# Three input stages: the power one round behind the variance, deeper rings, the mask read in place

## The reference, cut to what matters

```python
x = x + L0(_gn(x));  x = x + L1(_gn(x));  x = x + L2(_gn(x));  x = x + L3(_gn(x))

# L3, the others alike (L0 and L1 have no mask)
z_norm = layer_norm(z, norm_g, norm_b)
left  = (z_norm @ Wa + ba) * sigmoid(z_norm @ Wga + bga)
right = (z_norm @ Wb + bb) * sigmoid(z_norm @ Wgb + bgb)
left, right = left * mask[..., None], right * mask[..., None]
z_out = einsum('bikc,bjkc->bijc', left, right)
z_out = layer_norm(z_out, norm_out_g, norm_out_b)
return (z_out @ Wo + bo) * sigmoid(z_norm @ Wgo + bgo)
```

## Time and profile before

| | us |
|---|---|
| median of 3 runs | 1777.76 (1776.29 to 1778.16) |
| profiled execution | 1780.16 |
| its span, first to last instruction | 1778.4 |
| busy: PE, DVE, ACT, POOL | 1331.0, 1383.3, 1167.7, 1001.5 |

### The profile page before, as it was taken

How to read it: one execution, slowest core, us unless ns; L and a number is a source line. 1 busy time by engine, 2 the same in 40 slices (tenths; PEclk the granted TensorE clock), 3 DMA queues, 4 the chain that set the end, 5 groups by cost and what they waited for, 6 DMA issues and landing times.

```text
span 1778.4 us, 30667 instructions
## 1 busy us (share of the span) xinstructions
PE 1331.0 (75%) x9712; PEld 797.9 (45%) x9712; DVE 1383.3 (78%) x3708; ACT 1167.7 (66%) x2680; POOL 1001.5 (56%) x701
## 2 busy tenths in 40 slices
PE   5558888798688879798899657666675577778765
PEld 1123337665433349565677323333333233337654
DVE  6978871598688851898599899999999577761598
ACT  2358881598588851898343377777776288871598
POOL 7379960387699920687455214444445687740354
PEclk8879999899899999899899858989999799998789
DMA  7025436377545553677244124444445334435477
GB/s 263 0 78 119 120 88 155 99 222 208 142 107 119 120 120 77 182 227 208 89 110 113 33 54 110 105 108 107 106 109 119 96 100 107 100 78 133 135 256 249
DMA packets 408833, 225.53 MB, mean 127 GB/s; under 512 B 343456, under 2 KB 343776, under 8 KB 408672
## 3 DMA queue, kind: packets, MB, share of 16 engines
q1 hardware_dynamic: 270240, 185.81, 38.7%
q10 hardware_dynamic: 138432, 37.76, 9.1%
HBM read 114.97 MB, written 66.06 MB: 102 GB/s over the span
## 4 chain that ended last, share of the span: by engine, by line
issue 28%; DVE 21%; POOL 21%; ACT 16%; PE 12%; DMA 1%; SPq 0%; POOLq 0%; ACTq 0%; DVEq 0%
ACT work L1012 12%; POOL ln_s L514 6%; DVE stats L725 5%; PE ps L1131 5%; POOL work L506 4%; POOL work L520 4%; PE ps L1248 4%; POOL work L474 3%; POOL sg_all L549 2%; PE ps L1160 2%; DVE pairs L783 2%; ACT work L1025 2%; DVE stats L809 1%; DVE work L641 1%; ACT work L994 1%
## 5 line engine op out<-in xcount | busy, mean ns | idle before, releaser
L514 POOL TENSOR_TENSOR ln_s<-ln_s,half_power 128x8 f32<-128x8 f32 x216 | 356.4, 1650 | 355.7 <-DVE ln_s L734 305.2
L1173 PE MATMUL ps<-wfold,work 64*128 64x320 f32 x1728 | 342.6, 488 | 98.8 <-DVE pairs L783 52.8
L1131 PE MATMUL ps<-work,ones 128*128 128x512 f32 x504 | 280.6, 673 | 59.8 <-ACT work L970 49.5
L1012 ACT ACTIVATE work<-pairs,ln_s 128x64 f32<-128x64 f32 x648 | 263.4, 497 | 19.1 <-DVE ln_s L741 19.1
L1012 ACT ACTIVATE work<-work,ln_s 128x64 f32<-128x64 f32 x576 | 212.4, 430 | 95.4 <-DVE ln_s L741 95.2
L1173 PEld LDWEIGHTS ps<-wfold,work 64*128 64x128 f32 x1728 | 139.0, 190 | 270.6 <-DVE pairs L783 133.1
L783 DVE TENSOR_TENSOR pairs<-ps,work 128x256 f32<-128x256 f32 x288 | 169.0, 597 | 63.3 <-ACT work L1025 58.3
L1025 ACT ACTIVATE work<-ps 128x384 f32<-128x384 f32 x432 | 194.4, 476 | 4.9 <-PE ps L1173 3.8
L1160 PE MATMUL ps<-ident,work 128*128 128x128 f32 x864 | 147.7, 298 | 47.2 <-DVE work L752 28.8
L994 ACT ACTIVATE work<-ps 128x512 f32<-128x512 f32 x216 | 129.2, 598 | 72.1 <-PE ps L1160 70.5
L1072 ACT ACTIVATE pairs<-pairs,rescale 128x256 f32<-128x256 f32 x288 | 122.5, 498 | 71.3 <-DVE work L914 71.3
(11 more groups left out here) (148 smaller groups left out, 2636.0 us busy)
## 6 DMA issues: line engine op xcount, KB each, us to landing
work<-x_mid SPq DMA_DIRECT2D x144, 256.0 KB, 2.9
gate_dram<-work ACTq DMA_DIRECT2D x108, 256.0 KB, 2.8
work<-gate_dram SPq DMA_DIRECT2D x108, 256.0 KB, 3.2
work<-in_x_in SPq DMA_DIRECT2D x72, 256.0 KB, 2.9
work<-x_nat SPq DMA_DIRECT2D x144, 128.0 KB, 3.0
x_mid<-work SPq DMA_DIRECT2D x72, 256.0 KB, 2.6
work<-pairs SPq DMA_DIRECT2D x96, 96.0 KB, 3.0
work<-pairs ACTq DMA_DIRECT2D x96, 96.0 KB, 3.2
```

Of the source, the lines that this page charges most:

```text
L514: pool.tensor_tensor(ln_s[:, b, RSTD, :], ln_s[:, b, VAR, :], half_power[:, 0:U], ALU.pow)\
L1012: last = act.activation(dst[:, r % dst.shape[1], u * C:(u + 1) * C], src, ACT.Identity, scale=ln_s[:, b, RSTD, u:u + 1], bias=ln_s[:, b, S ...
L1131: last = pe.matmul(ps[:, bank, :], ones[:], src[:, b, :], start=first, stop=end, skip_group_check=True)
L1173: last = pe.matmul(ps[:, PAIR_BANKS[n % 3] + odd, 0:PROJ], xnT[rows, b, pair * P:(pair + 1) * P], wfold[rows, q, 0:PROJ], start=True, stop ...
```

## The change

- In the input stages `ln_moments` and `ln_var` get lead 4 (3 before), `scale` 5 (4), `centre` 6 (5). The power keeps lead 3, so that it handles a tile whose variance was made one round earlier.
- `normed` becomes a ring of six tiles, `stats` and `ln_s` have four sets. The guards are loosened accordingly: `centre` waits for tile t-6, power and shift for tile t-4. The output stages use the same helpers, with unchanged leads.
- To make room, the transposed tile has another place in the input stages (`xnT_in`) than in the output stages (`xnT_out`).
- The mask's scalar is read from `mask_sb` in place; copy, `mask_t` and semaphore go. An unused bf16 identity matrix goes as well.

```diff
-        xin, _, _, xn, xnT = (part(work, 1024 * k, ROW) for k in range(5))
-        normed = part(work, 1024, ROW, RING)
+        xin, normed = part(work, 0, ROW), part(work, 1024, ROW, NORM_RING)
+        xn, xnT_in = (part(work, 4096 + 1024 * k, ROW) for k in range(2))
...
-        mask_t = sb("mask_t", [P, 2, U])
-        stats = sb("stats", [P, 2, PAIRS, 6])
-        ln_s = sb("ln_s", [P, 2, 3, U])
+        stats = sb("stats", [P, RING, PAIRS, 6])
+        ln_s = sb("ln_s", [P, RING, 3, U])
...
-            pool.memset(ident16[:], 0.0).then_inc(s_const, 1)
...
                 if isinstance(t, int) and t == 0:
                     pool.wait_ge(gn_ready, l + 1)
-                wait_free(pool, xn_ready, tr_base(l, 0) + t - 3)
-                wait_free(pool, xn_act, tr_base(l, 0) + t - 3)
-                pool.tensor_tensor(tokens(normed[:, r, :]), tokens(xin[:, b, :]), over_tokens(gn_mean[:]), ALU.subtract)\
+                if t >= NORM_RING:
+                    pool.wait_ge(xn_ready, tr_base(l, 0) + t - NORM_RING + 1)
+                    pool.wait_ge(xn_act, tr_base(l, 0) + t - NORM_RING + 1)
+                pool.tensor_tensor(tokens(normed[:, t % NORM_RING, :]), tokens(xin[:, b, :]), over_tokens(gn_mean[:]), ALU.subtract)\
                     .then_inc(x_centred, 1)
...
             def token_rstd(l, side, t, b):
                 n = tr_base(l, side) + t
                 pool.wait_ge(var_ready, n + 1)
-                wait_free(pool, xn_ready, n - 1)
-                wait_free(pool, xn_act, n - 1)
-                pool.tensor_tensor(ln_s[:, b, RSTD, :], ln_s[:, b, VAR, :], half_power[:, 0:U], ALU.pow)\
+                wait_free(pool, xn_ready, n - 3)
+                wait_free(pool, xn_act, n - 3)
+                pool.tensor_tensor(ln_s[:, t % RING, RSTD, :], ln_s[:, t % RING, VAR, :], half_power[:, 0:U], ALU.pow)\
                     .then_inc(rstd_ready, 1)
...
-                    pipeline(pool, [(4, lambda t, b, r: scale(l, t, b, r), RING),
-                                    (5, lambda t, b, r: centre(l, t, b, r), RING),
+                    pipeline(pool, [(5, lambda t, b: scale(l, t, b)),
+                                    (6, lambda t, b: centre(l, t, b)),
                                     (3, lambda t, b: token_rstd(l, 0, t, b))])
...
                 dve.wait_ge(rstd_ready, n + 1)
-                wait_free(dve, xn_act, n - 1)
+                wait_free(dve, xn_act, n - 3)
...
-                if l == 3 and pair == 0:
-                    dve.tensor_copy(mask_t[:, b, :], mask_sb[:, cols(t)]).then_inc(mask_ready, 1)
-                    dve.wait_ge(mask_ready, t + 1)
...
-                            in0=ps[:, bank + u, 0:VALUES], scalar=mask_t[:, b, u0 + u:u0 + u + 1],
+                            in0=ps[:, bank + u, 0:VALUES], scalar=mask_sb[:, t * U + u0 + u:t * U + u0 + u + 1],
...
-                    pipeline(dve, [(3, lambda t, b, r: ln_moments(l, 0, t, b, r), RING),
+                    pipeline(dve, [(4, lambda t, b, r: ln_moments(l, 0, t, b, r), RING),
                                    (0, lambda t, b: store_pair(l, 0, t, b)),
                                    (2, lambda t, b: ln_shift(l, 0, t, b)),
-                                   (3, lambda t, b: ln_var(l, 0, t, b)),
+                                   (4, lambda t, b: ln_var(l, 0, t, b)),
```

More of the change, by code:

```diff
@@ L59 @@
 RING = 4
+NORM_RING = 6
 WHOLE = [(0, 1), (1, 6), (6, 12), (12, 18), (18, 24), (24, 30), (30, 36)]
@@ L138, in build @@
         xres, gate = part(work, 0, ROW, RING), part(work, 8192, ROW, RING)
-        xn_out = part(work, 2048, ROW, RING)
+        xn_out, xnT_out = part(work, 2048, ROW, RING), part(work, 4096, ROW)
         xnew, shifted, squares = (part(work, 5120 + 1024 * k, ROW) for k in range(3))
@@ L248, in build @@
          mlp_out_ready, mres_loaded, least_ready, sg_ready,
-         s_apart) = [sem(f"sem_{k}") for k in range(82)]
+         s_apart) = [sem(f"sem_{k}") for k in range(81)]
         x_loaded, gate_stored, xnew_stored, mres_loaded, qT_ready, hqT_ready = [
@@ L465, in _ @@
             pool.memset(gn_roots[:], 0.0).then_inc(s_const, 1)
-            pool.wait_ge(s_const, 7)
-            for m in (ident, ident16):
+            pool.wait_ge(s_const, 6)
+            for m in (ident,):
                 pool.affine_select(out=m[:], in_=m[:], compare_op=ALU.not_equal, fill=1.0, base=0,
@@ L702, in ln_pair, with of_stats @@
                 if side == 0:
-                    return normed[:, r, 2 * k * C:(2 * k + 2) * C].rearrange("p (e c) -> p c e", e=2)
+                    return normed[:, t % NORM_RING, 2 * k * C:(2 * k + 2) * C].rearrange("p (e c) -> p c e", e=2)
                 return pairs[:, 0, :, bass.ds(t * U + 2 * k, 2)]
-            def of_stats(b, what):
-                return stats[:, b, :, :].rearrange("p k (e s) -> p (k e) s", s=3)[:, :, what]
+            def of_stats(t, what):
+                return stats[:, t % RING, :, :].rearrange("p k (e s) -> p (k e) s", s=3)[:, :, what]
             def output_weights(q):
@@ L724, in ln_moments, with small @@
                 for k in range(PAIRS):
-                    last = dve.bn_stats(stats[:, b, k, :], ln_pair(side, t, r, k))
+                    last = dve.bn_stats(stats[:, t % RING, k, :], ln_pair(side, t, r, k))
                 last.then_inc(ln_step, 1)
-            def small(b, k):
-                return ln_s[:, b, k, :]
+            def small(t, k):
+                return ln_s[:, t % RING, k, :]
             def ln_var(l, side, t, b):
                 dve.wait_ge(ln_step, tr_base(l, side) + t + 1)
-                dve.tensor_scalar(small(b, VAR), of_stats(b, 2), C * LN_EPS, None, ALU.add).then_inc(var_ready, 1)
+                dve.tensor_scalar(small(t, VAR), of_stats(t, 2), C * LN_EPS, None, ALU.add).then_inc(var_ready, 1)
             def ln_shift(l, side, t, b):
@@ L739, in ln_shift @@
                 dve.wait_ge(rstd_ready, n + 1)
-                wait_free(dve, xn_act, n - 1)
-                dve.scalar_tensor_tensor(out=small(b, SHIFT), in0=of_stats(b, 1), scalar=-1.0, in1=small(b, RSTD),
+                wait_free(dve, xn_act, n - 3)
+                dve.scalar_tensor_tensor(out=small(t, SHIFT), in0=of_stats(t, 1), scalar=-1.0, in1=small(t, RSTD),
                                          op0=ALU.mult, op1=ALU.mult).then_inc(shift_step, 1)
@@ L751, in normalise @@
                 for u in range(DVE_TOKENS[l, side]):
-                    last = dve.tensor_scalar(dst[:, r % dst.shape[1], u * C:(u + 1) * C], src(u), small(b, RSTD)[:, u:u + 1],
-                                             small(b, SHIFT)[:, u:u + 1], ALU.mult, ALU.add)
+                    last = dve.tensor_scalar(dst[:, r % dst.shape[1], u * C:(u + 1) * C], src(u), small(t, RSTD)[:, u:u + 1],
+                                             small(t, SHIFT)[:, u:u + 1], ALU.mult, ALU.add)
                 last.then_inc(xn_ready, 1)
@@ L808, in h_moments @@
                 for k in range(PAIRS):
-                    last = dve.bn_stats(stats[:, b, k, :],
+                    last = dve.bn_stats(stats[:, t % RING, k, :],
                                         ps[:, CENTRED_BANK + b, 2 * k * C:(2 * k + 2) * C].rearrange("p (e c) -> p c e", e=2))
@@ L1012, in normalise @@
                     last = act.activation(dst[:, r % dst.shape[1], u * C:(u + 1) * C], src, ACT.Identity,
-                                          scale=ln_s[:, b, RSTD, u:u + 1], bias=ln_s[:, b, SHIFT, u:u + 1])
+                                          scale=ln_s[:, t % RING, RSTD, u:u + 1], bias=ln_s[:, t % RING, SHIFT, u:u + 1])
                 if 1 in halves:
@@ L1120, in _ @@
         def _(pe):
[L1121 removed]
+            pe.wait_ge(s_const, 7)
             pe.wait_ge(x_whole[0], 16)
@@ L1172, in project @@
                     rows = slice(C * odd, C * odd + C)
-                    last = pe.matmul(ps[:, PAIR_BANKS[n % 3] + odd, 0:PROJ], xnT[rows, b, pair * P:(pair + 1) * P],
+                    last = pe.matmul(ps[:, PAIR_BANKS[n % 3] + odd, 0:PROJ], xnT_in[rows, b, pair * P:(pair + 1) * P],
                                      wfold[rows, q, 0:PROJ], start=True, stop=True)
@@ L1247, in project_out @@
                 for k in range(PAIRS):
-                    last = pe.matmul(ps[:, b, k * P:(k + 1) * P], xnT[:, b, k * P:(k + 1) * P],
+                    last = pe.matmul(ps[:, b, k * P:(k + 1) * P], xnT_out[:, b, k * P:(k + 1) * P],
                                      w_out, start=True, stop=True)
```

29 lines of the change are left out of this document (13 added, 16 removed).

## The result

The changed kernel took 1785.57 us (median of 15 runs, 1780.8 to 1788.87), the kernel before 1776.29 in the same sessions (15 runs, 1771.32 to 1783.11). The ratio over all executions is 1.0047, with a 95% interval of 1.0033 to 1.0060: +8.3 us (5.9 to 10.7); the two medians lie 9.3 us apart. The forecast was 1782.4, slower by 4.7. The profiled execution took 1783.45 us, 3.3 more than that of before; the two profiled executions lie on opposite sides of their medians. The ratios leave out executions over 1.5% above the fastest of the same kernel: three of twelve in experiment 9, its profiled one among them, and one of seven in experiment 10.

What follows compares the result with a forecast made beforehand. It took a VectorE-ScalarE loop through the shift, not GpSimd, to bound the input stages. 7.35 - 1.06 - 6.3 + 4.7 = +4.7 us gave 1782.4 us, range 1775.0 to 1789.0.

Steps and rivals of the forecast that it cites:

- The ring: Input stages: VectorE-ScalarE loop through the shift sets tiles; 4.42 us kept in layers 0 and 1, 4.95 in layer 3.
- The second rival: Input stages: GpSimd's work holds VectorE's round; freeing it brings layers 0 and 1 to 4.10, -19.8; 1759.0 us; chance 0.10.
- The head: Start of each input stage: extra scaling and centring ahead of the first power, +2.45 us in each of three, +7.35.
- The tail: End of each input stage: one more round without moments, -0.32, -0.32 and -0.42 us, together -1.06.
- The mask: Layer 3's input stage: the mask copy and its wait leave VectorE's round, 0.19 us in some 33 rounds, -6.3.
- Catching up: Input stages after their start: GpSimd regains about a tile, its scaling and centring stalling VectorE's small instructions, +4.7 us.
- two hits a stage: Layers 0 and 1: two VectorE stalls each behind scaling or centring, 0.88 us apiece; a little over one in layer 3.
- the slide: Early tiles of each input stage: while GpSimd regains its place, its scaling and centring cross VectorE's instructions; +4.7 us.
- The sign that was given: Between the third and twelfth tile of each stage, one or two tiles take 0.5 to 1.1 us more.

Runs made afterwards that it cites:

- experiment 9: Changed kernel with GpSimd's scaling and centring back at leads 4 and 5; 1781.98 us, ratio 1.0014 against the kernel before.
- experiment 10: Kernel before with the mask read in place and, in the input stages, VectorE's variance and shift ahead of the first store; 1765.02 us, ratio 0.9929.
- experiment 5: Changed kernel with VectorE's shift at lead 3 in place of 2; 1764.78 us, ratio 0.9916 against the kernel before.
- experiment 6: Changed kernel with GpSimd scaling only 4 of 8 tokens of each tile in the input stages; 1779.64 us in one run.
- experiment 3: Changed kernel with VectorE's moments and variance back at lead 3; 1778.75 us, ratio 1.0005 against the kernel before.
- experiments 1 and 2: First: kernel before with only the mask read in place, 1768.96 us. Second: changed kernel with the mask copied again, 1793.56 us.
- the two looks: Two profiles of the changed kernel, the second with no edit; 1783.45 us for the first profiled execution, 1789.33 us for the second look's run.
- Experiment 4: Changed kernel with the old, tight waits on the normalisings in the output stages; 1783.83 us, ratio 1.0029 against the kernel before.
- experiment 7: Changed kernel with the shift at lead 3 behind VectorE's normalising, GpSimd's scaling and centring back at leads 4 and 5; 1759.97 us, ratio 0.9897.
- experiment 12: The kernel of experiment 10, with no edit, profiled a second time; 1764.56 us.

## Why the prediction was right, point by point

The sign and the range were right, the time 3.2 us low and the difference too small, +4.7 for +8.3. By its own steps:

- *The ring.* Right. The steady tiles stayed at 4.42 and went to 4.94 in layer 3; the shift taken out of the ring shortened it (4.28, experiment 5), half the scaling did not (experiment 6). The second rival, with its term of -19.8, is gone.
- *The head.* Right in size: forecast 2.45 a stage, measured 2.41 (first sigmoid at 16.42 for 14.01). GpSimd's leads alone make it (experiment 3); VectorE's alone would make 1.21 (experiment 9, layer 0).
- *The tail.* Forecast -1.06, measured about -0.8: in layers 0 and 1 one more tile of 4.11, but the next took 4.18 in place of 4.09; in layer 3 one of 4.54 in place of 4.94.
- *The mask.* Too small: -6.3 forecast, -7.8 measured in both orders (experiments 1 and 2). The steady tiles had it right; the term left out that the copy itself could be held. In the trace of before it is held once, for 0.79 us at 1420.55, in the tile of 5.78; why the next took 5.63 was not followed.
- *Catching up.* Right in kind, too small: +4.7 forecast; from the tile times, some +2.4 in layer 0 (0.54, 1.07 and 0.80 over 4.42), +2.3 in layer 1 and +1.35 in layer 3, about +6.0. I had two hits a stage at 0.88 each; layer 0 has six stretched instructions within 15 us, since scaling and centring can hold two normalisings in turn (from 131.30) or shift and variance in turn (from 135.33). Number and price of the hits were both wrong, in opposite directions, and that they nearly made up for each other is luck. The price was read from one tile of layer 1, 5.30 us, as that of the shift held at 500.62; the trace of before shows a second instruction held in it, the normalising of 497.01. ScalarE waited 0.78 us for the transposes behind that one, where the next tile has 0.37, and 0.66 for the shift, where the next has 0.18: 0.41 and 0.48 make the 0.88. In the slide the six hits of layer 0 cost 2.4, 0.4 each. The cause was put half right: the full tile that GpSimd has to gain comes from VectorE's moments and variance moving ahead (experiment 9), and moving GpSimd's work alone starts no slide (experiment 3). The sign that was given, one or two long tiles a stage, held in layer 3 (5.99 and 5.33); layers 0 and 1 have three each.

```profile
497.01 1.09 DVE L752 TENSOR_SCALAR work<-work,ln_s 128x64 f32<-128x64 f32 x3
```

```profile
500.08 0.60 ACT L994 ACTIVATE work<-ps 128x512 f32<-128x512 f32 x1 [0.78 <-PE ps L1160]
...
501.72 0.77 ACT L1012 ACTIVATE work<-work,ln_s 128x64 f32<-128x64 f32 x2 [0.66 <-DVE ln_s L741]
```

Head 7.2, slide 6.0, tail -0.8, mask -7.8 make +4.6, against +4.9 measured in the stages and +4.7 forecast: the slide 1.3 too small and the mask's gain 1.5 too small cancelled, which is luck again. The +8.3 of the 15 executions is more than the +4.9 and +6.4 that the two looks show in the input stages. The 2 to 3 us between lie outside them or in the spread; outside the stages, two executions of the changed kernel differ by 4.4 us (1243.2 and 1247.6). Experiment 4 couldn't tell whether the output stages' looser waits have a part in it. One thing on record goes with it: of the 23 executions of the kernel before beside experiments 4, 6, 7 and 9, the one with the highest mean granted clock of TensorE, 0.920, took 1771.69 us, and the four at 0.906 took 1781.12 to 1782.50; all 23 had 0.9105 on the mean, the 15 of the changed kernel 0.9066. By the line through the 23 a clock lower by 0.004 goes with some 3 us (an estimate). Whether the clock is the cause or follows from what the change does isn't shown, and the rest stays open.

## What to carry to other kernels

Before moving work ahead on one engine, ask which engine will have to catch up, by how much a round, and across which instructions of another engine it will pass on the way. Count everything that the new order puts ahead of the first result of a stage; it is paid at each stage's start. And look for the ring that closes on itself rather than for the busiest engine: the cheap gain here was to take one 0.17 us instruction, the shift, out of it, once the power was a round early: 15.4 us of the stages between the changed kernel (538.4) and experiment 5 (523.0), heads included. Experiment 10 gets there with the leads of before, by moving variance and shift ahead of the first store (507.9 in its good execution), but not in every execution.

## What the runs showed of the hardware

- VectorE's 128x8 shift, variance and copy and its 128x64 normalising stand still while GpSimd scales or centres (128x512, 1.27 us) and end 0.02 to 0.06 us behind it. The moments (0.86 us for four) and the stores, which read PSUM, run on beside them. Beside a GpSimd power (128x8, 1.64 us) the normalisings run on the earlier trace rows, and so does the shift: in experiment 7 it lies beside the power in 93 cases and takes at most 0.17 us. The Trainium skill, SBUF — State Buffer, section "SBUF: two separate sides", has the loser fully blocked for the whole instruction, when the VectorE instruction has two inputs in SBUF, as the shift has, and GpSimd's reads SBUF: the rows agree for scaling and centring, and not for the power.
- I hadn't expected a second rhythm that lasts. With no change in the program, a layer ran for 13 tiles (experiment 12, 5.3 us on the mean) or for most of its 36 (experiment 9, 5.5) in place of 4.26 or 4.42, and the granted clock in the two stretches above (0.96 and 1.00) differs far less than the tile times do.
- An order can be faster on the mean and less even: experiment 10 spread over 26 us in seven executions, experiment 7 over 9 in six.
